# Gathers that add expert rows into the residual, and the norms' two small sums moved from DVE to POOL

## The chip, the cores and the metric

The kernel runs on 1 core of one Trainium2 chip. The metric is the device time of one execution in microseconds; where several executions were timed, it is their median. TensorE (PE) has its own weight loads beside it (PEld). The other engines are VectorE (DVE), ScalarE (ACT), GpSimd (POOL) and SyncE (SP), which here only issues DMAs.

## The reference

Two decoder layers over x, 8 sequences of 256 tokens of 256 numbers, each sublayer followed by a norm. Cut to what matters:

```python
x = _layernorm(x + _L0_attn_ref(x, ...))      # mixing over tokens by a decay matrix
x = _layernorm(x + _L0_xattn_ref(x, ctx_512, ...))   # 16 heads, causal
x = _layernorm(x + _L0_ffn_ref(x, ...))       # 8 experts, top 1, and a shared expert
x = _layernorm(x + _L1_attn_ref(x, ...))      # FFT of the heads, normalized, cumsum, inverse
x = _layernorm(x + _L1_xattn_ref(x, ctx_512, ...))   # 16 heads in a latent space, rope
x = _layernorm(x + _L1_ffn_ref(x, ...))       # ternary weights, gated, rms norm
def _layernorm(x, axis=-1, eps=1e-05):
    m = jnp.mean(x, axis=axis, keepdims=True)
    v = jnp.var(x, axis=axis, keepdims=True)
    return (x - m) / jnp.sqrt(v + eps)
def _L0_ffn_ref(...):
    expert_idx = jnp.argmax(logits, axis=-1)
    for e in range(n_experts):
        out = out + jnp.where(m, h @ down_w[e], 0.0)
    return (out + shared).reshape(S, B, Dm)
```

## The kernel before

A unit is one sequence (256 tokens, two tiles of 128) in one layer. Units 0 to 7 are the first layer, 8 to 15 the second. Five lanes of on-chip buffers hold first-layer units and four lanes hold second-layer units, so that unit u of the second layer uses lane u % 4 and unit 12 takes the buffers of unit 8. Buffers are named after the areas that hold them: "wide" is lanes 0 and 1 of the second layer (and before that the experts' and other weights), "first" is lanes 2 and 3.

Between the layers stand the experts. Each first-layer unit writes its tokens, scaled by the router's score, into the DRAM tensor sent_rows, sorted by expert, and writes its residual plus the shared expert into x_mid (st_mid). When all tokens are sent, 23 tiles of 128 rows are loaded (x_ld), run through the expert of the tile (x_t, x_gu, x_h, x_b, x_dn, x_out) and stored to the DRAM tensor made_rows (x_st). A table of each token's row in made_rows is worked out on DVE (tb_tok).

A second-layer unit then starts. SP loads its rows of x_mid into B.y (ld). POOL issues two indirect DMAs (gt, line 2321), one for each tile of 128 tokens, which gather the tokens' rows of made_rows into B.got. Both wait until all of made_rows and x_mid has landed ("opened"). DVE adds the two (res with n = 0, line 1969) and the norm follows.

A norm (ln, ln_pow, ln_x) is split over three engines. DVE takes the statistics of both tiles (bn_stats, line 1927; bn_aggr, line 1930) into B.mv, whose third column holds eps, then two small reductions give variance + eps (line 1932) and minus the mean (line 1933). POOL raises to the power -0.5 (line 2275) and multiplies (line 2277). ACT applies scale and shift (line 1647). There are 48 norms: two for each first-layer unit (n = 0, 1), four for each of the second layer (n = 0 to 3).

No order is written out by hand. lay_plan describes every part (name, unit, index) with its engine, a length in units of 10 ns, what must come before it, a rank and its PSUM banks. settle(banks, passes, seed) lays all parts out on the engines in simulated time, with a random shake of the ranks by the seed, repeats it for the given number of passes and keeps the layout that ends first. Each engine then runs its parts in that order, and a part waits by semaphores for those before it; an instruction that waits holds up all that stands behind it on its engine. "AIR" is the flight of a DMA. keep_warm puts dummy matmuls (line 1461) into the planned gaps of TensorE of 0.8 us and more, from 9 us on. In the middle of the program the weights of the second layer are prepared: "h" steps fold attention weights (ha is line 1144), "f" steps make the ternary weights (f_sc, f_gt on DVE, f_q on POOL, lines 2332 to 2339).

## Time and profile before

| | us |
|---|---|
| median of 3 runs | 640.63 (639.15 to 644.22) |
| profiled execution | 638.61 |
| its span, first to last instruction | 637.3 |
| mean granted TensorE clock | 0.979 of full speed |

The profile is of one execution. Its span runs from the first to the last instruction; the execution's own time has 1.3 us more around it. Busy time counts an engine's instructions without those that only wait, branch or issue DMAs from SP. TensorE's matmuls overlap, so a duration of one matmul is longer than the step from one to the next. In the tables by stage the busy time of each engine is followed by the number of its instructions; in the order of time a bracket holds the engine's idle time before the instruction and what ended it.

### The profile page before, as it was taken

Reading aid. Unit: us, or ns where it says so; the run is one execution under the profiler, and the core shown is the slowest. Engines: PE = TensorE matmul, PEld = TensorE weight load, DVE = VectorE, ACT = ScalarE, POOL = GpSimd, SP = SyncE. Lnnn points to the kernel's source line nnn. Section 1 sums busy time; section 2 is a strip of 40 time slices with the busy share of each in tenths; the row PEclk is TensorE's granted clock in tenths of the full one; section 3 lists DMA queues with packets and bytes.
Section 4 is the critical chain, followed back from the end, with each engine's and each line's share of the span. In section 5 each row is a group of like instructions: output and inputs, shape, how many; then the busy total and the mean of one; then the engine's idle time right before and its main releaser. Section 6 shows DMA issues by size and latency. Waiting matters only on the chain. (4 is left out here: it accounts for less than half of the span.)

```text
span 637.3 us, 14620 instructions
## 1 busy us (share of the span) xinstructions
PE 574.4 (90%) x5400; PEld 445.5 (70%) x5400; DVE 480.8 (75%) x1286; ACT 386.7 (61%) x826; POOL 374.3 (59%) x468
## 2 busy tenths in 40 slices
PE   5789989988889799876989999999999999999995
PEld 4656767767666465553546888886788768889894
DVE  4673767776688798866779877697988997876656
ACT  3668667667766455541765565665747655655763
POOL 3436445556783267578998654572675634333896
PEclk9999999999899899998989999999999999999999
DMA  9753221102455244426211000001000000000001
GB/s 257 231 147 80 60 84 60 42 19 68 141 145 163 76 124 150 126 92 182 79 38 35 1 2 2 7 29 35 1 9 27 14 21 2 1 2 2 2 1 67
DMA packets 50418, 41.75 MB, mean 66 GB/s; under 512 B 15642, under 2 KB 48924, under 8 KB 50332
## 3 DMA queue, kind: packets, MB, share of 16 engines
q1 hardware_dynamic: 46444, 35.08, 18.6%
q0 software_dynamic: 1536, 4.20, 2.1%
q10 hardware_dynamic: 2368, 1.54, 0.9%
q8 instruction: 44, 0.72, 0.5%
q14 instruction: 26, 0.21, 0.1%
HBM read 31.49 MB, written 10.35 MB: 66 GB/s over the span
## 5 line engine op out<-in xcount | busy, mean ns | idle before, releaser
L1821 DVE TENSOR_TENSOR first<-bank,first 128x512 f16<-128x512 f32 (+3 forms) x141 | 76.1, 556 | 22.5 <-ACT first L1656 5.9
L2297 POOL TENSOR_TENSOR first<-first 128x512 f16<-128x512 f32 x44 | 51.9, 1181 | 42.4 <-ACT first L1708 32.6
L1077 PE MATMUL bank<-c_identity,first 128*128 128x128 f32 (+1 forms) x353 | 58.9, 284 | 9.2 <-DMA first<-in_x 3.1
L1070 PE MATMUL bank<-wide,first 128*128 (+4 forms) x199 | 54.2, 282 | 11.9 <-DVE first L1821 5.1
L1077 PEld LDWEIGHTS bank<-c_identity,first 128*128 128x128 f32 (+1 forms) x353 | 40.3, 141 | 20.3 <-DMA first<-in_x 3.7
L1071 PE MATMUL bank<-wide,first 128*128 (+4 forms) x199 | 53.8, 280 | 0.0
L1072 PE MATMUL bank<-wide,first 128*128 (+4 forms) x199 | 52.9, 279 | 0.0
L2275 POOL TENSOR_TENSOR first<-first,minus_half 128x2 f32<-128x2 f32 x30 | 21.6, 719 | 46.5 <-DVE first L1933 46.5
L1077 PE MATMUL bank<-c_identity,wide 128*128 128x128 f32 (+3 forms) x203 | 34.1, 291 | 9.2 <-DMA c_all_ones<-const_all_ones 7.1
L1821 DVE TENSOR_TENSOR wide<-bank,wide 128x512 f16<-128x512 f32 (+3 forms) x57 | 35.0, 635 | 9.0 <-ACT wide L1687 3.5
L1070 PEld LDWEIGHTS bank<-wide,first 128*128 128x128 f16 (+1 forms) x199 | 19.2, 98 | 24.6 <-issue 16.5
L1647 ACT ACTIVATE wide<-wide 128x256 f32<-128x256 f32 x32 | 17.4, 593 | 31.0 <-POOL wide L2277 30.9
L1077 PEld LDWEIGHTS bank<-c_identity,wide 128*128 128x128 f32 (+3 forms) x203 | 23.9, 146 | 16.2 <-DMA c_all_ones<-const_all_ones 7.1
L1700 ACT ACTIVATE first<-bank 128x512 f16<-128x512 f32 x44 | 26.2, 596 | 11.1 <-PE bank L1328 5.4
L1998 DVE TENSOR_REDUCE first<-bank 128x8 f32<-128x512 f32 x44 | 27.6, 681 | 6.1 <-PE bank L1290 3.7
L2332 POOL TENSOR_TENSOR wide<-wide 128x768 bf16<-128x768 bf16 x8 | 13.1, 1642 | 31.5 <-DVE wide L1919 31.5
L1494 PE MATMUL bank<-first,w_fgu 128*128 128x256 f16 x256 | 29.8, 273 | 0.6 <-DVE first L2219 0.6
L1494 PE MATMUL bank<-wide,w_fgu 128*128 128x256 f16 x256 | 30.1, 273 | 0.0
L2396 POOL TENSOR_TENSOR wide<-wide 128x512 f16<-128x512 f32 x16 | 18.6, 1161 | 19.0 <-ACT wide L1797 19.0
L1708 ACT ACTIVATE first<-bank 128x512 f32<-128x512 f32 x44 | 26.3, 597 | 5.7 <-POOL first L2297 5.5
L2297 POOL TENSOR_TENSOR wide<-wide 128x512 f16<-128x512 f32 x16 | 18.5, 1158 | 17.9 <-ACT wide L1708 15.4
L1070 PE MATMUL bank<-first,wide 128*128 128x256 f16 (+1 forms) x98 | 25.9, 271 | 2.4 <-DVE first L1821 2.4
(471 smaller groups left out, 2106.3 us busy)
## 6 DMA issues: line engine op xcount, KB each, us to landing
first<-sent_rows SPq DMA_DIRECT2D x20, 128.0 KB, 2.0
made_rows<-first SPq DMA_DIRECT2D x20, 128.0 KB, 1.8
wide<-in_L_ffn_gate_w SPq DMA_DIRECT2D x8, 256.0 KB
wide<-in_L_ffn_up_w SPq DMA_DIRECT2D x8, 256.0 KB
wide<-in_L_ffn_down_w SPq DMA_DIRECT2D x8, 256.0 KB
wide<-in_L_xattn_Wq SPq DMA_DIRECT2D x8, 256.0 KB
wide<-in_L_xattn_Wo SPq DMA_DIRECT2D x16, 128.0 KB
wide<-in_L_ffn_w_gate_up SPq DMA_DIRECT2D x8, 256.0 KB
```

The lines of the kernel that those rows point to most:

```text
L1070: mm(o, lhs[0], rhs[0], start=start, stop=False)
L1071: mm(o, lhs[0], rhs[1], start=False, stop=False)
L1072: return mm(o, lhs[1], rhs[0], start=False, stop=stop)
L1077: last = nc.tensor.transpose(view[0:m, c0:c0 + n], src, kc["identity" if dt == F32 else "identity_bf"][0:n, 0:n])
L1494: last = mm(b[:, n * S:(n + 1) * S], k.w_fgu[:, c, at:at + P], B.xT[part][:, c, :], start=(c == 0 and part == 0), stop=(c == C - 1 and par ...
L1700: fn(lane(u).ph[g % 2], scores(u, g)[:, :], ACT.Exp, scale=0.25 if u < NB else 1.0).then_inc(says("ex_h"), 1)
L1708: fn(lane(u).pf, scores(u, g)[:, :], ACT.Exp, scale=0.25 if u < NB else 1.0).then_inc(says("ex_f"), 1)
L1821: return V.tensor_tensor(lo, whole, hi, ALU.subtract)
L1998: V.tensor_reduce(o, b, AX.X, ALU.max).then_inc(says("max_v"), 1)
L2275: pool.step(G.tensor_tensor(B.rstd, B.rstd, k.minus_half, ALU.pow))
L2297: G.tensor_tensor(B.pl[r], B.pf, B.ph[r], ALU.subtract).then_inc(says("ex_l"), 1)
L2396: G.tensor_tensor(lo, B.hf, hi, ALU.subtract).then_inc(says("hf_lo"), 1)
```

## The change

The gathering transfers now add: with compute_op=ALU.add they add the rows of made_rows to what is in B.y. The tile B.got and the addition on DVE (line 1969) go, and the norm waits for the gathers themselves. A gather therefore waits on POOL until its unit's rows of x_mid have landed, and no longer for the addition of the unit that had the lane before. The loads of units 8 and 9 no longer wait for made_rows, but for the experts' last matmuls and for x_mid.

In 44 of the 48 norms DVE stops after bn_aggr; POOL then makes minus the mean (tensor_scalar) and variance + eps (tensor_tensor) ahead of its power. The first norms of units 8 to 11 keep the two reductions on DVE.

The plan's lengths of the norm's parts follow that, and the lengths of f_sc, f_gt, rt_xs, tb_tok and of the gather's flight are changed as well. settle takes 25 passes and seed 157 in place of 37 and 38. Since every engine's order comes out of settle, the order of the whole program is laid out anew.

```diff
@@ -111,6 +111,11 @@
 def was_in(n):
 
     return 3 if n < 3 else 4 if n == 3 else FIRST
+
+
+def sums_on_vector(u, n):
+
+    return NB <= u < NB + LANES and n == 0
 
 
 class Box:
@@ -307,8 +312,8 @@
         p.add(name + "_lo", u, g, lo_on, lo, [(name + "_hi", u, g)], rank)
 
     def norm(u, n, rank, summed="res"):
-        p.add("ln", u, n, "DVE", 130, [(summed, u, n), ("pm_pow", 0, 0)], rank)
-        p.add("ln_pow", u, n, "POOL", 100, [("ln", u, n)], rank)
+        p.add("ln", u, n, "DVE", 130 if sums_on_vector(u, n) else 100, [(summed, u, n), ("pm_pow", 0, 0)], rank)
+        p.add("ln_pow", u, n, "POOL", 100 if sums_on_vector(u, n) else 140, [("ln", u, n)], rank)
         p.add("ln_x", u, n, "ACT", 109, [("ln_pow", u, n)], rank)
 
 
@@ -386,8 +391,8 @@
             p.add("ld_f", 0, i, "SP", 140, freed, rank)
             p.add("in_f", 0, i, "AIR", 350, [("ld_f", 0, i)])
             p.add("f_16", 0, i, "ACT", 82, [("in_f", 0, i)], rank)
-            p.add("f_sc", 0, i, "DVE", 170, [("f_16", 0, i)], rank)
-            p.add("f_gt", 0, i, "DVE", 195, [("f_sc", 0, i)], rank)
+            p.add("f_sc", 0, i, "DVE", 185, [("f_16", 0, i)], rank)
+            p.add("f_gt", 0, i, "DVE", 186, [("f_sc", 0, i)], rank)
             for n2 in range(4):
                 p.add("f_q", 0, 4 * i + n2, "POOL", 164, [("f_q", 0, 4 * i + n2 - 1) if n2 else ("f_gt", 0, i)], rank)
             p.add("fw", 0, i, "PE", 46, [("f_q", 0, 4 * i + 3), ("in_const", 0, 0)], rank, 1, ("fw_c", 0, i))
@@ -444,7 +449,7 @@
         p.add("rt_top", u, 0, "DVE", 20, [("rt", u, 0)], k - 0.5)
         p.add("rt_gate", u, 0, "ACT", 20, [("rt_top", u, 0)], k - 0.5)
         p.add("rt_hot", u, 0, "DVE", 77, [("rt_top", u, 0), old("rk")], k - 0.5)
-        p.add("rt_xs", u, 0, "ACT", 140, [("rt_gate", u, 0)], k - 0.5)
+        p.add("rt_xs", u, 0, "ACT", 114, [("rt_gate", u, 0)], k - 0.5)
         before = [("rk_seen", u - 1, 0)] if u else []
         p.add("rk_seen", u, 0, "DVE", 35, [("rt_hot", u, 0)] + before, k - 0.5)
         p.add("rk", u, 0, "PE", 20, [("rt_hot", u, 0)] + before, k - 0.5, 1, ("rk_slot", u, 0))
@@ -470,7 +475,7 @@
     p.add("tb", 0, 0, "PE", 10, [("rk_seen", NB - 1, 0)], 6, 1, ("tb_cnt", 0, 0))
     p.add("tb_cnt", 0, 0, "DVE", 200, [("tb", 0, 0)] + over, 6)
     p.add("tb_tile", 0, 0, "DVE", 421, [("tb_cnt", 0, 0), ("in_tab", 0, 0)], 6)
-    p.add("tb_tok", 0, 0, "DVE", 498, [("tb_tile", 0, 0)] + [("rk_slot", u, 0) for u in every], 22)
+    p.add("tb_tok", 0, 0, "DVE", 560, [("tb_tile", 0, 0)] + [("rk_slot", u, 0) for u in every], 22)
     for n in range(NT):
         k = 10 + 0.1 * n
         o = n - ELANES if n >= ELANES else None
@@ -499,9 +504,10 @@
             return (name, o, g) if o is not None else None
 
         gate = [("x_in_st", n, 0) for n in range(NT)] + [("in_mid", v, 0) for v in every]
-        p.add("gt", u, 0, "POOL", 200, gate + [("tb_tok", 0, 0), old("res", 0)], k)
-        p.add("in_gt", u, 0, "AIR", 200, [("gt", u, 0)])
-        p.add("ld", u, 0, "SP", 45, gate + [("in_mid", i, 0), old("ln_x", 3)], k)
+        p.add("gt", u, 0, "POOL", 200, gate + [("tb_tok", 0, 0), ("in", u, 0)], k)
+        p.add("in_gt", u, 0, "AIR", 220, [("gt", u, 0)])
+        over = [("x_dn", NT - 1, 0)] + [("in_mid", v, 0) for v in every] if i < 2 else gate
+        p.add("ld", u, 0, "SP", 45, over + [old("ln_x", 3)], k)
         p.add("in", u, 0, "AIR", 250, [("ld", u, 0)])
         p.add("ld_ctx", u, 0, "SP", 90, gate + [old("rope")], k)
         p.add("in_ctx", u, 0, "AIR", 250, [("ld_ctx", u, 0)])
@@ -510,8 +516,7 @@
         p.add("kd_lo", u, 0, "POOL", 43, [("kd_hi", u, 0)], k)
         chain("kt", u, 0, [("rope", u, 0), old("sc", 3)], k, pe=20, hi=29, lo=28)
 
-        p.add("res", u, 0, "DVE", 70, [("in_gt", u, 0), ("in", u, 0)], k)
-        norm(u, 0, k)
+        norm(u, 0, k, "in_gt")
         chain("turn", u, 0, [("ln_x", u, 0)], k)
         for t in range(T):
             p.add("ft", u, t, "PE", 136, [("turn_lo", u, 0), ("pd_lo", 0, 0), ("pd_lo", 0, 1)], k, 1, ("ft_raw", u, t) if t else ("nr", u, 0))
@@ -568,7 +573,7 @@
         p.add("res", u, 3, "DVE", 122, [("rm_pow", u, 0), ("proj", u, 3)], k)
         norm(u, 3, k)
         p.add("st", u, 0, "SP", 45, [("ln_x", u, 3)], k)
-    p.settle(8, 37, 38)
+    p.settle(8, 25, 157)
     p.keep_warm(80, 0.7, 900)
     return p
 
@@ -808,7 +813,7 @@
             return v if dt == F32 else v.bitcast(dt)
 
         tn = "p (t n) -> p t n"
-        B.x, B.y, B.got = (tile([T, D]) for m in range(3))
+        B.x, B.y = (tile([T, D]) for m in range(2))
         B.xT = (tile([C, S], F16), tile([C, S], F16))
         B.ctx, B.kv, B.rot = (tile([DC]) for m in range(3))
         B.kv2 = tile([P])
@@ -988,7 +993,12 @@
                 sp.wait_ge(*done("rt_xs", u - FIRST))
             load(B.x, unit_rows(A["x"], u), dma["x"][u % FIRST])
         else:
-            opened(u)
+            if u < NB + 2:
+                sp.wait_ge(*done("x_dn", NT - 1))
+                for n in range(FIRST):
+                    sp.wait_ge(dma["mid"][n], 16 * turns_of(n))
+            else:
+                opened(u)
             if u >= NB + LANES:
                 sp.wait_ge(*done("ln_x", u - LANES, 3))
             load(B.y, unit_rows(k.x_mid, u - NB), dma["x"][u % LANES])
@@ -1920,7 +1930,10 @@
 
     def ln(u, n):
         B = lane(u)
-        dve.wait_ge(*done("proj" if u < NB and n < 2 else "res", u, n))
+        if u >= NB and n == 0:
+            dve.wait_ge(dma["got"][u % LANES], 32 * visit(u))
+        else:
+            dve.wait_ge(*done("proj" if u < NB and n < 2 else "res", u, n))
         dve.wait_ge(*done("pm_pow", 0))
         y = summed_rows(k, u, n)
         for t in range(T):
@@ -1928,6 +1941,9 @@
         dve.step(last)
         for t in range(T):
             last = V.bn_aggr(B.mv[:, t, 0:2], B.stats[:, t, :])
+        if not sums_on_vector(u, n):
+            last.then_inc(says("ln"), 2)
+            return
         dve.step(last)
         V.tensor_reduce(B.rstd, B.mv[:, :, 1:3], AX.X, ALU.add).then_inc(says("ln"), 1)
         V.tensor_reduce(B.mean, B.mv[:, :, 0:1], AX.X, ALU.add, negate=True).then_inc(says("ln"), 1)
@@ -1963,10 +1979,6 @@
         if u < NB:
             dve.wait_ge(*done("proj", u, n))
             last = V.scalar_tensor_tensor(B.y, bank("proj", u, n)[:, :].rearrange(tn, t=T), 0.5, B.x, ALU.mult, ALU.add)
-        elif n == 0:
-            dve.wait_ge(dma["x"][u % LANES], 16 * (turns_of(u % LANES) + visit(u)))
-            dve.wait_ge(dma["got"][u % LANES], 32 * visit(u))
-            last = V.tensor_tensor(B.y, B.y, B.got, ALU.add)
         elif n < 3:
             dve.wait_ge(*done("proj", u, n))
             last = V.scalar_tensor_tensor(B.y, bank("proj", u, n)[:, :].rearrange(tn, t=T), 1.0, B.x, ALU.mult, ALU.add)
@@ -2272,6 +2284,10 @@
         B = lane(u)
         pool.wait_ge(says("ln"), 2 * k.plan.place[("ln", u, n)] - 1)
         pool.wait_ge(*done("pm_pow", 0))
+        if not sums_on_vector(u, n):
+            pool.wait_ge(says("ln"), 2 * k.plan.place[("ln", u, n)])
+            G.tensor_scalar(B.mean, B.mv[:, :, 0], -1.0, None, ALU.mult)
+            pool.step(G.tensor_tensor(B.rstd, B.mv[:, :, 1], B.mv[:, :, 2], ALU.add))
         pool.step(G.tensor_tensor(B.rstd, B.rstd, k.minus_half, ALU.pow))
         pool.wait_ge(says("ln"), 2 * k.plan.place[("ln", u, n)])
         G.tensor_tensor(B.shift, B.mean, B.rstd, ALU.mult).then_inc(says("ln_pow"), 1)
@@ -2315,11 +2331,10 @@
         B, i = lane(u), u - NB
         opened()
         pool.wait_ge(*done("tb_tok", 0))
-        if u >= NB + LANES:
-            pool.wait_ge(*done("res", u - LANES, 0))
+        pool.wait_ge(dma["x"][u % LANES], 16 * (turns_of(u % LANES) + visit(u)))
         for s in range(T):
-            G.indirect_dma_start(B.got[:, s, :], None, k.made[:, :], bass.IndirectOffsetOnAxis(ap=k.made_at[:, i * T + s:i * T + s + 1], axis=0)
-                                 ).then_inc(dma["got"][u % LANES], 16)
+            G.indirect_dma_start(B.y[:, s, :], None, k.made[:, :], bass.IndirectOffsetOnAxis(ap=k.made_at[:, i * T + s:i * T + s + 1], axis=0),
+                                 compute_op=ALU.add).then_inc(dma["got"][u % LANES], 16)
 
     def f_q(u, n):
         i, step = n // 4, n % 4
```

## Rows read from the trace of the kernel before

**Rows 1.** The page, part 1: busy time, share of the span, instructions.
```profile
PE 574.4 (90%) x5400; PEld 445.5 (70%) x5400; DVE 480.8 (75%) x1286; ACT 386.7 (61%) x826; POOL 374.3 (59%) x468
```

**Rows 2.** Table: stretch, length, busy PE, PEld, DVE, ACT, POOL, clock, DMA, GB/s.
```profile
48.00:208.00 160.00, 142.76 (x1810) 112.64 (x1807) 114.26 (x355) 111.59 (x253) 92.38 (x105) 0.98 0.29 86
208.00:288.00 80.00, 69.33 (x441) 42.27 (x441) 64.31 (x138) 41.84 (x114) 45.40 (x30) 0.98 0.37 111
288.00:304.00 16.00, 10.66 (x44) 5.92 (x44) 10.16 (x27) 3.03 (x8) 14.22 (x14) 0.79 0.62 181
304.00:352.00 48.00, 43.31 (x288) 27.19 (x285) 39.17 (x108) 30.15 (x67) 43.84 (x92) 0.96 0.18 51
352.00:624.00 272.00, 267.28 (x2506) 225.59 (x2505) 214.17 (x555) 169.25 (x321) 153.02 (x176) 1.00 0.03 9
```

**Rows 3.** The same table for line 1461, the dummy matmuls, alone.
```profile
48.00:208.00 160.00, 6.61 (x22) 2.29 (x22) 0.98 0.29 86
...
288.00:304.00 16.00, 4.92 (x23) 2.06 (x21) 0.79 0.62 181
304.00:352.00 48.00, 6.42 (x20) 2.32 (x20) 0.96 0.18 51
```

**Rows 4.** TensorE's waits, 304 to 352 us: total, times, longest.
```profile
PE bank L1476 <- POOL wide L2376: 2.1, 1, 2.1
...
PE bank L1077 <- POOL wide L2385: 0.8, 1, 0.8
```

**Rows 5.** DVE by time: start, duration, instruction, [idle before, until].
```profile
293.31 0.69 DVE L1969 TENSOR_TENSOR wide<-wide 128x512 f32<-128x512 f32 x1 [2.86 <-DMA wide<-made_rows,made_at]
...
294.83 0.25 DVE L1930 BATCH_NORM_AGGREGATE mv<-stats 128x2 f32<-128x6 f32 x2
...
295.19 0.14 DVE L1933 TENSOR_REDUCE wide<-mv 128x2 f32<-128x2 f32 x1
296.02 1.62 DVE L1969 TENSOR_TENSOR wide<-wide 128x512 f32<-128x512 f32 x1 [0.69 <-DMA wide<-made_rows,made_at]
```

**Rows 6.** POOL in order of time, where the second layer begins.
```profile
289.32 1.11 POOL L2321 DMA_INDIRECT wide<-made_rows,made_at  x1 [0.30 <-issue]
...
295.44 1.64 POOL L2332 TENSOR_TENSOR wide<-wide 128x768 bf16<-128x768 bf16 x1
297.04 1.19 POOL L2275 TENSOR_TENSOR wide<-wide,minus_half 128x2 f32<-128x2 f32 x1
...
325.99 1.07 POOL L2321 DMA_INDIRECT wide<-made_rows,made_at  x1 [0.17 <-issue]
...
346.58 0.94 POOL L2321 DMA_INDIRECT first<-made_rows,made_at  x1 [0.30 <-issue]
```

**Rows 7.** TensorE in order of time: the weight fold ahead of unit 8.
```profile
298.26 3.73 PE L1144 MATMUL bank<-wide 128*96 128x256 f32 x8 [5.34 <-DMA wide<-in_L_xattn_W_qr]
```

**Rows 8.** Landing times: gathers (line 2321), loads into lanes 2 and 3.
```profile
DMA to landing us min/median/max: 2.7/3.2/4.5
...
first<-x_mid SPq DMA_DIRECT2D x4, 256.0 KB, 3.7
```

**Rows 9.** Unit 13's load and addition by time; table by stretch.
```profile
434.83 0.36 SPq L897 DMA_DIRECT2D wide<-x_mid  x1
...
438.53 0.68 DVE L1969 TENSOR_TENSOR wide<-wide 128x512 f32<-128x512 f32 x1
...
432.00:464.00 32.00, 29.75 (x251) 22.37 (x250) 26.62 (x73) 22.70 (x47) 17.38 (x21) 1.00 0.06 18
...
507.00:528.00 21.00, 19.68 (x174) 15.10 (x172) 19.02 (x52) 11.81 (x23) 6.96 (x11) 1.00 0.09 26
```

**Rows 10.** The last norm, in order of time.
```profile
632.48 0.25 DVE L1930 BATCH_NORM_AGGREGATE mv<-stats 128x2 f32<-128x6 f32 x2
...
633.00 0.69 POOL L2275 TENSOR_TENSOR first<-first,minus_half 128x2 f32<-128x2 f32 x1 [1.34 <-DVE first L1933]
633.78 0.20 POOL L2277 TENSOR_TENSOR first<-first 128x2 f32<-128x2 f32 x1
```

## The prediction

> **What bounds the kernel now.** I read the engines' busy time first, then a table of busy time by stage, then what ended TensorE's idle time, then the order of time on POOL and DVE where the second layer begins. TensorE is busy for 574.4 of 637.3 us, DVE for 480.8 [rows 1], so whatever is saved must show as TensorE time that is now idle or filled with the dummy matmuls of line 1461. The stages differ widely [rows 2]. From 352 to 624 us TensorE is idle for only 272.0 - 267.28 = 4.7 us: in that stretch less work on DVE or POOL is worth at most that. From 48 to 208 us it is idle for 17.2 us and does 6.6 us of dummies [rows 2, 3]. From 288 to 304 us it is idle for 5.3 us and does 4.9 us of dummies at a granted clock of 0.79, and from 304 to 352 us 4.7 and 6.4 us, while POOL is busy for 43.84 of 48 us [rows 2, 3]. Two of the waits of that last stretch end on POOL, 2.1 and 0.8 us [rows 4]. So the beginning of the second layer is the place where this change can earn something, and POOL is its fullest engine there.
>
> **The change, part by part.** I make the sum against the profiled execution, 638.6 us with a span of 637.3 us; the median of the runs shown is 640.63, 2.0 us more. I carry the difference over to that median.
>
> *The addition in the gather.* Eight DVE additions (line 1969) go. One takes 0.69 us when it runs undisturbed and 1.62 us beside POOL [rows 5]. Eight of them are 5.5 to 13 us of DVE time; off the path they are worth nothing, since TensorE has other work. On the path is the first one: the gathers of unit 8 let it start at 293.31 and its norm starts 0.04 us after it, so the norm may start 0.7 us sooner. There is a second effect. The sums for POOL are ready at 295.33, but POOL took up a ternary-fold step of 1.64 us at 295.44, and the power came at 297.04 and lasted 1.19 us [rows 5, 6]. With the norm 0.7 us sooner the power is ready at 294.6, while POOL is still issuing gathers (until 295.4), and goes before that step if the order says so: 297.04 - 295.44 = 1.6 us. I take 1.6 us in all for the entry. Its bounds: nothing, because TensorE's first matmuls for unit 8 stand behind a weight fold, which waited 5.34 us for a DMA until 298.26; and 5.3 us, that whole wait, if the new order lets the unit's work fill it [rows 7].
>
> The Trainium skill (SBUF — State Buffer, "SBUF: two separate sides") says that a DVE instruction with two SBUF inputs and a POOL instruction that reads SBUF exclude each other for their whole length. The 0.69 against 1.62 us, and the power's 1.19 against 0.69 us, agree with it. By that rule the removed additions also give POOL time back, and the added POOL sums take some from such DVE instructions; neither enters the sum here.
>
> *The gather now waits for its rows' other half, not for an old tile.* Before, the gathers of units 12 to 15 were issued from 325.99 to 347.5 us, in the stretch where POOL is full: 8 issues of about 1.0 us and 0.3 us between the two of a pair, some 9 us [rows 6]. Now each waits for x_mid to land in its lane's tile, which waits for the end of the lane's previous unit (412 us and later). POOL loses 9 of its 43.84 us there. It takes on the sums of the few second norms that fall there, about 1 us. I take the two waits on POOL of rows 4 as what is won, 2.9 us. Bounds: nothing, if what is next is DVE (39.17 of 48 us), and 11.1 us, if all idle and dummy time of this stretch became work [rows 2, 3].
>
> *The price: a lane starts later.* Unit 13's load was issued at 434.83 and its addition began at 438.53, 3.7 us later [rows 9]. Now two gathers follow the load: from the first issue to the landing of the second is 1.3 us to the second issue and 293.31 - 289.32 = 4.0 us from there, 5.3 us; the addition of 0.7 us and its gap go: +4.6 us per lane, plus up to 1.3 us if POOL is busy. It happens at four lanes (units 12 to 15). What covers it is the ready work of the other three lanes. At units 12 and 14 TensorE is full. At units 13 and 15 it is not: it idles 32.0 - 29.75 = 2.25 us from 432 to 464 and 21.0 - 19.68 = 1.3 us from 507 to 528 [rows 9]. If the cover fails, one such start costs 4.6 us. I take a sixth of that at each of the two, 1.5 us together, because even there TensorE waits only in pieces shorter than a restart. Units 10 and 11 load behind the gate as before, and unit 10's gathers come on POOL after four others of some 1.3 us each, longer than the 3.7 us in which its load landed [rows 6, 8]; units 8 and 9 are loaded before the gate. So at the entry the new wait costs nothing. On SP the early loads stand ahead of stores that need a later step of the same tile anyway.
>
> The new wait sits on POOL's queue. Behind it stand the splits, squares and powers of the other three lanes, and TensorE waits for those. The planner gives a load 0.45 + 2.5 us, while the loads of units 10, 11, 14 and 15 took 3.7 us to land [rows 8]: where the order leaves no room, POOL stands still for up to 0.8 us. This is in the 1.5 us, and its failure is part of the third rival.
>
> *What the add itself costs.* No row shows an accumulating transfer. The nearest is the same gather without the add: 2.7 to 4.5 us to landing, 3.2 in the median [rows 8], and about 1 us of POOL per issue. Below: nothing more. Above: the destination is read as well, as long again as a landing, +3.2 us at the entry and at each restart, and POOL's issue doubled. I take nothing more, since a gather of 128 KB is mostly a fixed delay; the upper end goes into the range.
>
> *The small sums.* 44 of 48 norms lose two DVE reductions: from the end of the aggregates to the end of the second reduction, 295.08 to 295.33, 0.25 us of DVE each and 11 us in all [rows 5]. Each gains two POOL instructions of 128x2, like the product at 633.78 (0.20 us), and a wait between, 0.08 us as before that product: 0.35 to 0.48 us, 15 to 21 us in all [rows 10]. On the path of one norm the power began 0.27 us after the aggregates (632.73 to 633.00), now the two instructions and the wait come before it, 0.35 to 0.48 us, and a signal under 0.1 us: about 0.5 us, +0.23 us. In the tail this counts once, and three norms ahead of it on DVE give back 0.17 us or so where they are in series: nothing. In the first layer (13 norms from 48 to 208 us) DVE is busy for 114 and POOL for 92 of 160 us: 3 us less on the fuller, 5 us more on the emptier engine, at most 13 x 0.23 = 3.0 us of latency if no lane covered another. I take nothing; the bounds are -3 and +3 us.
>
> *The order.* The planner gets other durations (also for steps that the code leaves alone: f_sc, f_gt, rt_xs, tb_tok), dependences, seed and passes, so every engine's order is drawn anew. What this does can't be worked out; what it can move can: the 23.9 us idle and dummy from 48 to 208 us and the 10.3 us from 288 to 304 us [rows 2, 3]. I take zero.
>
> Sum: -1.6 - 2.9 + 1.5 = -3.0 us; 638.6 becomes 635.6, and at the level of the median 640.6 - 3.0 = 637.6 us.
>
> **The rivals.**
> *The entry and the new order pay in full.* POOL's freed 9 us and the 5 us of the entry bring 5 and 4 us instead of 2.9 and 1.6, and the order fills a tenth (3 us) of the 34 us above, with 1.5 us of restarts: -10.5 us, 630 us. For it: a fold that waits 5.34 us ahead of ready work is an accident of order. Against it: another accident can take its place.
> *All of it hidden.* TensorE's gaps are refilled by waits on DVE and ACT: 640.6 us. For it: DVE at 39 of 48 us next to POOL.
> *The restarts are exposed (the other side).* At units 13 and 15 the three other lanes run dry and TensorE waits the whole 4.6 us each, 9.2 us, and the two others cost 1 us each: 11.2 - 4.5 = +6.7 us, 647 us. It decides from the point where the three lanes hold less than 4.6 us of ready matmuls at a restart. For it: TensorE waits there already. Against it: from 352 to 624 us all four starts together go with 4.7 us of idle time.
> *The accumulating gather is slow.* The Trainium skill (DMA: Bandwidth & Descriptors, "Rules for kernel authors") says that an accumulating DMA reads its destination and writes it later, so each gather would carry a further trip; no row here can show it. Worked from rows: +3.2 us at the entry and, at two restarts, 3.2 us more each: +9.6 - 3.0 = +6.6 us, again 647 us.
>
> **How the numbers follow.** A measurement of this kernel tells about 1% from no change (6.4 us). Forecast 0.40; paid in full 0.24; all hidden 0.14; restarts exposed or the gather slow 0.22. Faster by over 1% (under 634.2): all but a little of the second case and a part of the forecast's spread, 0.30. Slower (over 647.0): half of the last case and a larger draw of the order, 0.20. Same: 0.50. The range 628 to 648 takes in both neighbours and leaves out an order that moves more than a third of the 34 us. The likeliest case alone spans 634 to 641.
>
> **What would show it.** POOL's busy time from 304 to 352 us falls by some 8 us and its part of TensorE's waits there is gone; no gather stands between unit 11's and 410 us. The first norm of unit 8 starts as its gather lands. Each later lane's first norm starts 8 to 9 us after its load is issued (3.7 before), and TensorE's idle time from there on stays near 5 us; over 10 us there means that the third rival is true. A gather that lands later than 4.5 us after its issue means the fourth. If 48 to 288 us is shorter or longer by more than 3 us, it is the order that has moved the time, and my sum is right or wrong by luck.

## The result and the profile after

The changed kernel is slower. Its time is 1.0095 of the time before (95% interval 1.0073 to 1.0116; medians 648.47 and 642.90 us over 17 runs each). I had forecast 3 us less; it is 6 us more. The profiled execution took 648.99 us, its span is 647.7 us, where the one of before had 637.3.

The page after, part 1, and the stages of the same table as [rows 2] (stretch, length, busy time of PE, PEld, DVE, ACT and POOL with their instructions, granted clock, DMA share, GB/s):

```profile
PE 576.5 (89%) x5398; PEld 445.1 (69%) x5398; DVE 461.7 (71%) x1190; ACT 385.4 (59%) x826; POOL 400.4 (62%) x556
```
```profile
48.00:208.00 160.00, 145.09 (x1785) 112.26 (x1782) 116.00 (x340) 108.77 (x252) 89.54 (x119) 0.99 0.29 86
...
304.00:352.00 48.00, 42.11 (x307) 28.05 (x304) 38.48 (x108) 31.14 (x67) 42.66 (x92) 0.96 0.14 29
352.00:624.00 272.00, 258.03 (x2345) 214.63 (x2344) 196.60 (x483) 158.65 (x304) 157.25 (x212) 0.97 0.06 13
```

DVE has 19 us less work and POOL 26 us more [rows 1]. From 352 to 624 us TensorE is idle for 272.0 - 258.03 = 14.0 us, where it was 4.7 [rows 2], and its mean granted clock there is 0.97, where it was 1.00.

The time was lost late. In POOL's order of time, the first gather of the second layer and the first norm on DVE:

```profile
280.21 1.65 POOL L2336 DMA_INDIRECT wide<-made_rows,made_at  x1 [2.56 <-DMA made_rows<-first]
282.16 1.55 POOL L2336 DMA_INDIRECT wide<-made_rows,made_at  x1 [0.30 <-issue]
...
286.79 0.75 DVE L1940 BATCH_NORM_STATS2 stats<-wide 128x6 f32<-128x256 f32 x2 [1.16 <-DMA wide<-made_rows,made_at]
```

The first gather stands at 280.2 us, where it stood at 288.0:

```profile
288.00 1.02 POOL L2321 DMA_INDIRECT wide<-made_rows,made_at  x1 [1.47 <-DMA made_rows<-first]
```

Until then the changed kernel is 7.8 us ahead in this pair of profiles. From there to the end it takes 647.7 - 280.2 = 367.5 us, before 637.3 - 288.0 = 349.3: 18.2 us more. How far ahead a kernel is at the first gather changes from one execution to the next by some 5 us (the table of places below), so the two numbers are good to about that.

What the gathers' line shows, with the durations of the issue on POOL, and the queue of software-made descriptors on the page (packets, MB, share of 16 engines), first of the kernel after, then of before:

```profile
L2336 POOL DMA_INDIRECT wide<-made_rows,made_at x8: 1537/1600/2130, 280.2 to 456.1; - x8
...
DMA to landing us min/median/max: 3.7/4.0/5.6
```
```profile
q0 software_dynamic: 3072, 4.20, 3.3%
```
```profile
q0 software_dynamic: 1536, 4.20, 2.1%
```

An adding gather keeps POOL for 1.60 us, where a plain one kept it for 1.00, and lands 4.0 us after its issue in the median, where it was 3.2 [rows 8]. The bytes are the same; the packets of that queue have doubled.

### The profile page after: what moved, and what is told of

Its sections match the earlier page's. It is cut to its first block, busy times and chain, and to the rows that moved or that the text cites. A ratio compares the mean times of both kernels' runs of the same rounds, so it can differ in the third digit from the quotient of the medians.

```text
span 647.7 us, 14587 instructions
## 1 busy us (share of the span) xinstructions
PE 576.5 (89%) x5398; PEld 445.1 (69%) x5398; DVE 461.7 (71%) x1190; ACT 385.4 (59%) x826; POOL 400.4 (62%) x556
## 3 DMA queue, kind: packets, MB, share of 16 engines
q1 hardware_dynamic: 46444, 35.08, 18.2%
q0 software_dynamic: 3072, 4.20, 3.3%
q10 hardware_dynamic: 2368, 1.54, 0.9%
## 4 chain that ended last, share of the span: by engine, by line
PE 49%; POOL 14%; DVE 10%; ACT 7%; issue 5%; DMA 4%; SPq 1%; POOLq 0%; DVEq 0%; ACTq 0%
PE bank L1080 8%; PE bank L1082 7%; PE bank L1081 7%; PE bank L1504 6%; PE bank L1087 6%; PE bank L1262 4%; POOL first L2313 2%; POOL first L2336 2%; ACT first L1657 1%; DMA wide<-made_rows,made_at 1%; DVE stats L1940 1%; POOL wide L2336 1%; SPq L902 1%; PE bank L1154 1%; POOL first L2291 1%
## 5 line engine op out<-in xcount | busy, mean ns | idle before, releaser
L1087 PE MATMUL bank<-c_identity,first 128*128 128x128 f32 (+2 forms) x353 | 56.6, 281 | 6.9 <-DVE first L2010 2.3
L1080 PE MATMUL bank<-wide,first 128*128 (+4 forms) x199 | 53.0, 276 | 9.0 <-DVE first L1831 4.2
L1081 PE MATMUL bank<-wide,first 128*128 (+4 forms) x199 | 52.8, 275 | 0.0
L1087 PEld LDWEIGHTS bank<-c_identity,first 128*128 128x128 f32 (+2 forms) x353 | 39.4, 139 | 19.0 <-ACT first L1657 5.9
L1082 PE MATMUL bank<-wide,first 128*128 (+4 forms) x199 | 52.1, 275 | 0.0
L1710 ACT ACTIVATE first<-bank 128x512 f16<-128x512 f32 x44 | 25.9, 594 | 20.5 <-PE bank L1338 11.6
L1504 PE MATMUL bank<-wide,w_fgu 128*128 128x256 f16 x256 | 31.4, 279 | 0.6 <-DVE first L2034 0.6
L1657 ACT ACTIVATE first<-first 128x256 f32<-128x256 f32 x32 | 17.4, 592 | 21.8 <-POOL first L2293 21.8
L2289 POOL TENSOR_SCALAR first<-mv 128x2 f32<-128x2 f32 x28 | 6.9, 248 | 37.9 <-DVE mv L1943 37.8
L2411 POOL TENSOR_TENSOR wide<-wide 128x512 f16<-128x512 f32 x16 | 19.2, 1197 | 17.3 <-ACT wide L1807 17.3
L1504 PEld LDWEIGHTS bank<-wide,w_fgu 128*128 128x128 bf16 x256 | 25.4, 100 | 4.2 <-DVE first L2034 0.9
```

Of the source, the lines that this page charges most:

```text
L1080: mm(o, lhs[0], rhs[0], start=start, stop=False)
L1081: mm(o, lhs[0], rhs[1], start=False, stop=False)
L1082: return mm(o, lhs[1], rhs[0], start=False, stop=stop)
L1087: last = nc.tensor.transpose(view[0:m, c0:c0 + n], src, kc["identity" if dt == F32 else "identity_bf"][0:n, 0:n])
L1504: last = mm(b[:, n * S:(n + 1) * S], k.w_fgu[:, c, at:at + P], B.xT[part][:, c, :], start=(c == 0 and part == 0), stop=(c == C - 1 and par ...
L1657: last = fn(B.x[:, t, :], y[:, t, :], ACT.Identity, bias=B.shift[:, t:t + 1], scale=B.rstd[:, t:t + 1])
```

## The experiments

Each was compared with the kernel before on its own chip, so the ratios are to be compared, not the medians. Names that begin with b_ stand for the kernel before with an edit, those that begin with a_ for the changed kernel with an edit. Every engine keeps the order of that kernel, but for the gathers that b_late, b_add and a_early move on POOL and the addition that b_add takes out of DVE's order. b_seed42, a_told and c_got have orders of their own.

| kernel | ratio to before | 95% interval |
|---|---|---|
| changed | 1.0095 | 1.0073 to 1.0116 |
| b_sums: small sums on POOL | 1.0082 | 1.0051 to 1.0113 |
| b_sums2: the same, second layer only | 1.0023 | 0.9999 to 1.0048 |
| b_late: plain gathers, issued late | 1.0227 | 1.0178 to 1.0277 |
| b_add: adding gathers, issued late | 1.0369 | 1.0315 to 1.0423 |
| b_seed42: another order only | 0.9991 | 0.9955 to 1.0027 |
| a_plain: nothing added | 0.9899 | 0.9864 to 0.9935 |
| a_add8: added for units 8 to 11 only | 0.9952 | 0.9923 to 0.9980 |
| a_got: plain gather to its own tile, DVE adds | 0.9986 | 0.9968 to 1.0004 |
| a_early: the same, gathers early | 0.9983 | 0.9956 to 1.0009 |
| a_vec: changed, sums on DVE | 1.0091 | 1.0063 to 1.0119 |
| a_pad: a_plain with POOL held | 1.0090 | 1.0057 to 1.0124 |
| a_pad_after: the same, behind the pair | 1.0069 | 1.0037 to 1.0100 |
| a_told: the planner knows the gather's lengths | 1.0027 | 1.0007 to 1.0046 |
| c_got: plain gather, sums on POOL, planned anew | 0.9944 | 0.9912 to 0.9975 |

Ratios say what a kernel costs. Where it loses the time is read from places that all the kernels have: the start of the first gather, the start of unit 12's load of x_mid on SP (which waits for the end of unit 8) and the end of the span. One profiled execution of each, in us:

| kernel | first gather | load of unit 12 | end | gather to load | load to end |
|---|---|---|---|---|---|
| before | 288.0 | 412.7 | 637.3 | 124.7 | 224.6 |
| b_late | 292.3 | 413.9 | 659.0 | 121.7 | 245.1 |
| changed | 280.2 | 404.6 | 647.7 | 124.4 | 243.1 |
| a_plain | 283.5 | 402.6 | 633.9 | 119.1 | 231.3 |
| a_add8 | 282.8 | 406.9 | 639.3 | 124.1 | 232.5 |
| a_got | 282.7 | 404.3 | 641.6 | 121.6 | 237.3 |
| a_early | 279.7 | 405.3 | 636.7 | 125.6 | 231.4 |
| a_pad | 283.7 | 409.1 | 646.5 | 125.4 | 237.4 |
| a_pad_after | 285.4 | 410.8 | 645.9 | 125.5 | 235.1 |

b_late runs the same work in the same order as before up to the first gather, and gets there 4.3 us later; the kernels from changed to a_pad_after do the same work up to it, but for a store of a constant, and lie 5.7 us apart. The first column is therefore not to be read as an effect of an edit.

**One part of the change at a time, in the order of before.** b_sums:

```diff
+        if not sums_on_vector(u, n):
+            last.then_inc(says("ln"), 2)
+            return
...
+            G.tensor_scalar(B.mean, B.mv[:, :, 0], -1.0, None, ALU.mult)
+            pool.step(G.tensor_tensor(B.rstd, B.mv[:, :, 1], B.mv[:, :, 2], ALU.add))
```

> The kernel before, in its own order on every engine, with one part of the change: the two small sums of 44 of the 48 norms go from DVE to POOL. Theory 'sums' (they lengthen the norm's path and load POOL): 3 to 6 us slower than before. Theory 'gather' (the adding gather is what costs) and theory 'order' (the new order of all engines is what costs): within 1.5 us of before, with DVE busy about 10 us less and POOL about 20 us more.

It is 0.8% slower, so in this order the theory 'sums' holds. I then left the sums of the first layer on DVE:

```diff
-    return NB <= u < NB + LANES and n == 0
+    return u < NB or (u < NB + LANES and n == 0)
```

> The kernel before in its own order with the small sums on POOL only in the 28 norms of the second layer that the change moves; the 16 norms of the first layer stay on DVE. If each moved norm costs alike: 28 of 44 of the 5.0 us, 3.2 us slower than before. If the cost lies in the first layer, where TensorE waits on short chains (the profile's gate to the second layer came 5.7 us later there): within 1 us of before.

1.0023 is between the two forecasts, 0.5% and nothing. The larger part of the cost seems to come from the 16 norms of the first layer (the intervals of the two kernels, 0.51 to 1.13% and 0.0 to 0.48%, just fail to overlap). The traces can't show where: the first gather moves by 4.3 us without any edit (b_late).

b_add has the other part of the change: adding gathers, waits and loads as in the change, the DVE addition taken out of the order, the gathers of units 12 to 15 moved:

```diff
+        for u in range(NB + LANES, 2 * NB):
+            order = self.order["POOL"]
+            order.remove(("gt", u, 0))
+            landed = self.ends[("in", u, 0)]
+            at = next(n for n, k in enumerate(order) if self.starts[k] >= landed)
+            order.insert(at, ("gt", u, 0))
```

> The kernel before, in its own order, with the other part of the change: the gathers add into B.y, wait for the load of x_mid, and the addition on DVE is gone; the gathers of units 12 to 15 stand on POOL where their load has landed by the plan; the loads of units 8 and 9 wait for the last matmuls of the experts only. Theory 'gather': 5 to 9 us slower than before, with a gather's issue at 1.6 us of POOL and TensorE idle for 10 us or more from 352 to 624 us (before 4.7). Theory 'order': within 2 us of before.

3.7% slower, far more than either theory said. b_late has only the move of the gathers:

> The kernel before, in its own order, but the gathers of units 12 to 15 (still plain, into their own tile, added by DVE) are issued on POOL only where the load of their unit has landed by the plan, instead of at 326 to 347 us. It frees about 9 us of POOL where the second layer begins. If POOL's load there was worth the 2.9 us of the prediction: 2 to 3 us faster than before. If not (the stretch is held by chains that POOL's load doesn't touch): within 1 us. It also holds the late issue alone: slower by 2 us or more would mean that the late gather costs even without the add.

It is itself 2.3% slower. So the late place alone explains most of b_add in an order that was laid out for early gathers. The addition stands in DVE's order where its operands had always been there; now DVE stands still with everything behind it. The line of the addition in b_late:

```profile
its engine sat idle before it (us, times) until:
  DMA first<-made_rows,made_at: 8.3, 3
  DMA wide<-made_rows,made_at: 7.9, 2
```

This is 16.2 us, where the gathers made DVE wait 3.5 us in two waits at the entry before.

Did the relief of POOL that I had counted on come? The busy times of the stretch of [rows 2] in b_late seem to say no:

```profile
304.00:352.00 48.00, 43.46 (x285) 27.19 (x284) 39.15 (x108) 32.03 (x72) 40.07 (x88) 0.97 0.10 29
```

POOL is busy for 3.8 us less than before, TensorE for 0.15 us more. But a busy time holds the dummies too, and does not say how far the kernel has come. The order is the same in both, so the same instruction can be looked up in both. Two of POOL's instructions, one ahead of the gathers' old place and one ahead of unit 12's load, before and then in b_late:

```profile
321.39 0.31 POOL L2347 MEMSET first<- 128x256 bf16 x1
410.58 0.69 POOL L2275 TENSOR_TENSOR wide<-wide,minus_half 128x2 f32<-128x2 f32 x1 [0.43 <-DVE wide L1933]
```
```profile
326.21 0.31 POOL L2365 MEMSET first<- 128x256 bf16 x1
411.80 0.69 POOL L2293 TENSOR_TENSOR wide<-wide,minus_half 128x2 f32<-128x2 f32 x1 [0.43 <-DVE wide L1951]
```

From one to the other it takes 89.19 us before and 85.59 us in b_late: with the gathers gone the stretch is 3.6 us shorter. The relief came, and a little more than the forecast 2.9 us. What b_late loses it loses behind it, 20.5 us from unit 12's load to the end. Looked up in the same way, the loss comes in four steps, one at each restart of a lane: 8.9, 4.0, 4.3 and 3.2 us.

**What the add costs.** a_plain overwrites B.y with the gathered rows; the addition is left out:

```diff
-                                 compute_op=ALU.add).then_inc(dma["got"][u % LANES], 16)
+                                 ).then_inc(dma["got"][u % LANES], 16)
```

> The changed kernel in its order, but the gathers overwrite B.y instead of adding to it, so the expert rows are not added to the residual (that part of the result is left out). All waits and places are those of the changed kernel. It measures what the add itself costs. Theory 'gather, by its price': issue back at 1.0 us of POOL, landing back at about 3.2 us, 3 to 5 us faster than the changed kernel (644 to 645 where the changed one has 648). Theory 'gather, by its place' (the chain load, then gather, is what costs) and theory 'order': within 1.5 us of the changed kernel.

0.9899 against 1.0095: the add in the transfer costs 2.0%, some 12.6 us, more than the theory 'gather, by its price' had said. It is more than the whole loss. a_got does the addition on DVE again; its gathers go to a tile of their own and no longer wait for the load:

```diff
-        pool.wait_ge(dma["x"][u % LANES], 16 * (turns_of(u % LANES) + visit(u)))
+        if u >= NB + LANES:
+            pool.wait_ge(says("ln"), 2 * k.plan.place[("ln", u - LANES, 0)])
...
+            dve.wait_ge(dma["x"][u % LANES], 16 * (turns_of(u % LANES) + visit(u)))
             dve.wait_ge(dma["got"][u % LANES], 32 * visit(u))
+            dve.step(V.tensor_tensor(B.y, B.y, B.got, ALU.add))
```

> The changed kernel in its own order on every engine, but with the addition taken out of the transfer: the gathers stand in the same places of POOL's order, are plain, go to a tile of their own and don't wait for the load; DVE adds the two right ahead of the unit's first norm. Theory 'price of the add' (the issue at 1.6 instead of 1.0 us of POOL and the later landing cost the 13 us that the run without the add regained): 636 to 639 us, of which 1 to 2 us are the eight additions on DVE, so faster than the changed kernel by 1.5 to 2% and faster than before by some 0.6%. Rival 'less work of any kind' (the run without the add was fast because nothing at all was added): 643 us or more.

0.9986: better than the changed kernel by 1.1%, which is less than expected, since the eight additions on DVE, less what the dropped wait may bring, cost 0.9% against a_plain, not 0.2%. With the same order on every engine, the addition is cheaper on DVE than in the transfer. Where the transfer's price arises:

```diff
-                                 compute_op=ALU.add).then_inc(...)
+                                 **({"compute_op": ALU.add} if u < NB + LANES else {})).then_inc(...)
```

> The changed kernel, but only the gathers of units 8 to 11, at the start of the second layer, add; those of units 12 to 15 are plain and their addition is left out. The profiles of the plain and the adding version stand 5 us apart by unit 12's start and 12 us more between there and the end (3.3 of it an earlier gate in one of them). Theory 'it costs at every lane's start': a little over a third of the 2%, 0.996 to 0.999 of the time before. Theory 'it costs at the entry, where POOL is full': 1.004 or more.

0.9952, just below the range of the first theory: of the 2.0% about 0.5% arise at the four starts of the entry and 1.4% at the four restarts. The table of places agrees: from the first gather to unit 12's load the adding gathers take 5.3 us more than plain ones in the changed kernel and 5.0 us in a_add8, and from there to the end 11.8 us, where a_add8, plain again, takes 1.2 us more. It costs at every start, and more at the restarts.

**Issue or landing.** a_pad holds POOL behind each plain gather:

```diff
+            pool.step(G.tensor_tensor(k.pad[1], k.pad[0], k.minus_half, ALU.pow))
```

> The changed kernel with the gathers plain (the addition left out, as in the run that took 0.990 of the time before), and behind each gather's issue a piece of useless POOL work of 0.7 to 0.8 us on tiles of its own. It gives POOL the time of the adding issue (1.6 for 1.0 us), a little more, and the second gather of a pair the same delay, but leaves the transfers plain. Theory 'POOL's time is the price of the add': 1.005 to 1.013 of the time before, nearly all of the 2% between the plain and the adding gather. Theory 'the transfers' own delay is the price' (they land 3.7 us or more after their issue, before 2.7): 0.990 to 0.995.

1.0090 (with the addition left out, as in a_plain and in the next kernel): time on POOL alone brings the whole price back. But the padding delays the second gather too, and in the trace a pair with it takes 1.6 us more of POOL than a plain pair, where the adding pair takes 1.2 us more. So both pieces went behind the second gather:

> As the run with useless POOL work behind each gather's issue (1.009 of the time before), with the same work, but both pieces behind the second gather of a pair, so that the pair is issued and lands as early as the plain one. Theory 'the chain to the landing of the second gather is the price' (0.45 us or more later per pair): back to 0.990 to 0.994. Theory 'POOL's queue is the price' (what stands behind the pair is late by 1.5 us): 1.004 to 1.010.

1.0069: with the pair as early as the plain one, 1.7% are still there. Scaled from 1.6 to 1.2 us a pair, POOL's queue explains about 1.3 of the 2.0%, some 8 us; this is an estimate, and the intervals allow 0.4% either way. The rest is open between the later landing and the width of the intervals.

The restart of unit 14 shows how 0.6 us an issue come out at the end. POOL's order of time in a_plain, then in the changed kernel:

```profile
482.37 1.09 POOL L2336 DMA_INDIRECT first<-made_rows,made_at  x1 [0.17 <-issue]
483.76 0.95 POOL L2336 DMA_INDIRECT first<-made_rows,made_at  x1 [0.30 <-issue]
...
489.54 0.72 POOL L2422 TENSOR_TENSOR first<-first 128x256 f32<-128x256 f32 x1
```
```profile
490.95 1.69 POOL L2336 DMA_INDIRECT first<-made_rows,made_at  x1 [0.18 <-issue]
492.94 1.55 POOL L2336 DMA_INDIRECT first<-made_rows,made_at  x1 [0.30 <-issue]
...
499.31 0.72 POOL L2422 TENSOR_TENSOR first<-first 128x256 f32<-128x256 f32 x1
```

From the first issue to the last sum of another lane's squares: 7.17 us there, 8.36 here, 1.2 us more. Four full-width POOL instructions of other lanes stand between, and none of them makes it up. The third of them, again a_plain first:

```profile
487.08 1.15 POOL L2313 TENSOR_TENSOR wide<-wide 128x512 f16<-128x512 f32 x1
```
```profile
496.26 1.74 POOL L2313 TENSOR_TENSOR wide<-wide 128x512 f16<-128x512 f32 x1
```

TensorE's order of time there, a_plain first as before:

```profile
488.34 0.22 PE L1363 MATMUL bank<-wide 128*128 128x130 f16 x1 [0.47 <-issue]
490.31 0.61 PE L1513 MATMUL bank<-one,first 128*128 128x1 f32 x4 [1.14 <-POOL first L2422]
```
```profile
498.10 0.22 PE L1363 MATMUL bank<-wide 128*128 128x130 f16 x1 [1.65 <-issue]
500.08 1.01 PE L1513 MATMUL bank<-one,first 128*128 128x1 f32 x4 [1.14 <-POOL first L2422]
```

The first of the two gaps has grown by the same 1.2 us. The profile names nothing that ended it, but in both kernels it ends 0.1 us after the POOL instruction above (488.23 and 498.00 us). Then comes a second loss. TensorE's busy time and granted clock in stretches of 4 us, a_plain first:

```profile
487.60:491.60 4.00, 2.39 (x27) 1.00 0.00 0
491.60:495.60 4.00, 3.99 (x43) 1.00 0.00 0
```
```profile
496.00:500.00 4.00, 1.28 (x16) 0.92 0.05 7
500.00:504.00 4.00, 3.92 (x19) 0.50 0.00 0
504.00:508.00 4.00, 4.00 (x33) 0.72 0.00 0
508.00:512.00 4.00, 3.27 (x42) 1.00 0.02 6
```

Behind the longer gaps the granted clock falls to 0.50, the lower level of 1.2 GHz, and is back at 2.4 GHz only after 504 us. By the mean of 0.61 TensorE does 8 x (1 - 0.61) = 3.1 us less in those 8 us. In the changed kernel this happens three times between 416 and 508 us, in a_plain never. Summed over stretches of 4 us from 352 to 624 us, and estimating what the clock takes as each stretch's length times the missing share of the clock, the changed kernel loses 14.0 us to idle time and 6.9 us to the clock, a_plain 9.0 and nothing, a_pad 13.4 and 1.7, a_got 12.1 and 3.4. A fall of the clock is thus not bound to the add: a_pad is as slow as the changed kernel with fewer of them, and a_got has one and is 1.1% faster.

**The chain of load and gather.** a_early is a_got with the plain gathers of units 12 to 15 moved forward on POOL, three pairs to 352 to 359 us and one to 389 us:

```diff
+        for u, ahead in ((12, ("kd_lo", 12, 0)), (13, ("kd_lo", 12, 0)), (14, ("kd_lo", 12, 0)), (15, ("ss", 8, 2))):
+            order.remove(("gt", u, 0))
+            order.insert(order.index(ahead) + 1, ("gt", u, 0))
```

> The kernel with a separate addition on DVE in the order of the changed kernel (it took 0.9986 of the time before), with the gathers of units 12 to 15 issued in POOL's idle time near 355 us instead of behind their loads; they can be, since they go to their own tile. A lane's first norm then waits for the load alone, and no adding transfer is used. Theory 'the chain load, then gather, costs at each restart': 2 to 4 us faster, 0.993 to 0.996 of the time before, and faster than both kernels. Rival 'the order was laid out for the later norm, so an earlier one finds its engines busy': within 1 us, 0.997 to 1.000.

0.9983 beside 0.9986: no gain in sum. But it isn't that nothing happened. The same three instructions of POOL in a_got and then in a_early, one ahead of the gathers' new place, one ahead of unit 12's load, and the last:

```profile
352.38 1.16 POOL L2394 TENSOR_TENSOR first<-first 128x512 f16<-128x512 f32 x1
401.69 0.23 POOL L2291 TENSOR_SCALAR wide<-mv 128x2 f32<-128x2 f32 x1 [2.92 <-DVE mv L1945]
638.12 0.20 POOL L2295 TENSOR_TENSOR first<-first 128x2 f32<-128x2 f32 x1
```
```profile
349.39 1.16 POOL L2407 TENSOR_TENSOR first<-first 128x512 f16<-128x512 f32 x1
402.74 0.23 POOL L2304 TENSOR_SCALAR wide<-mv 128x2 f32<-128x2 f32 x1 [2.90 <-DVE mv L1958]
633.22 0.20 POOL L2308 TENSOR_TENSOR first<-first 128x2 f32<-128x2 f32 x1
```

From the first to the second a_early takes 53.35 us, a_got 49.31: eight gathers on POOL there cost 4.0 us, so its time there was not idle, as I had taken it. From the second to the third it takes 230.48 us, a_got 236.43: the late place had cost 6.0 us. Of these the clock has 1.7 and 3.4 us by the estimate above. So the chain of load and gather does cost at the restarts, 6 us in this order and 20.5 us in one that was laid out for early gathers (b_late), and the early place costs nearly as much on POOL.

**The sums in the changed order.** a_vec takes them back to DVE in all norms:

> The changed kernel in its own order, but all norms' small sums on DVE as before. Theory 'the sums on POOL lengthen each norm' (as in the order of before, where they cost 5 us): 3 to 5 us faster than the changed kernel, 643.5 to 645.5 us. Rival 'this order was laid out for them': within 1.5 us of the changed kernel.

1.0091 beside 1.0095: the rival holds. Here they cost nothing that the intervals show, 0.2 to 0.3% each.

**The order.** b_seed42 changes two numbers:

```diff
-    p.settle(8, 37, 38)
+    p.settle(8, 20, 42)
```

> The kernel before with nothing changed but the seed and the passes of the plan (seed 42, 20 passes): another order of every engine, whose planned end is 645.0 us against 643.6. It measures what a redrawn order alone does. If the plan's end tells the time: 1.002. If an order is worth what I allowed in the prediction (a tenth to a third of the idle time before the second layer): 0.99 to 1.015.

No difference within 0.4%. a_told gives the planner the gather's real lengths:

```diff
-        p.add("gt", u, 0, "POOL", 200, gate + ...)
-        p.add("in_gt", u, 0, "AIR", 220, [("gt", u, 0)])
+        p.add("gt", u, 0, "POOL", 350, gate + ...)
+        p.add("in_gt", u, 0, "AIR", 300, [("gt", u, 0)])
...
-    p.settle(8, 25, 157)
+    p.settle(8, 24, 293)
```

> The changed kernel, with the adding gather's real lengths given to the planner (3.5 us of POOL for the pair and 3.0 us of flight, instead of 2.0 and 2.2) and a seed and passes chosen by the plan's own end. The plan ends at 646.9 us (645.2 by the old lengths, 643.6 for the kernel before). Theory 'the cost is that the order doesn't know the real lengths': 640 to 644 us. Theory 'the cost is in the work and the chain themselves': 646 to 650 us.

1.0027, between the two theories: 0.7% of the time goes when the order knows the lengths, though the plan itself ends 1.7 us later. That it is the lengths and not merely another draw of the order isn't shown; the one draw tried alone (b_seed42) moved nothing. The rest stays in the work.

**A version that beats both.** c_got keeps the sums on POOL, has plain gathers that may be issued early and an addition on DVE as a part of its own, and a plan with measured lengths:

```diff
-        p.add("gt", u, 0, "POOL", 200, gate + [("tb_tok", 0, 0), ("in", u, 0)], k)
-        p.add("in_gt", u, 0, "AIR", 220, [("gt", u, 0)])
+        p.add("gt", u, 0, "POOL", 235, gate + [("tb_tok", 0, 0), old("res", 0)], k)
+        p.add("in_gt", u, 0, "AIR", 200, [("gt", u, 0)])
...
+        p.add("res", u, 0, "DVE", 110, [("in_gt", u, 0), ("in", u, 0)], k)
+        norm(u, 0, k)
...
-    p.settle(8, 25, 157)
+    p.settle(8, 26, 436)
```

> The small sums on POOL as in the change, but the gathers plain, to their own tile and free to be issued early, the addition a part of its own on DVE, and the plan laid out anew with the measured lengths of both (2.35 us of POOL, 2.0 us of flight, 1.1 us of DVE); its planned end is 644.3 us (before 643.6). Theory 'only the adding transfer and lengths that the plan doesn't know cost, the rest is neutral': 0.993 to 1.001 of the time before. Rival 'sums on POOL cost in any order': 1.005 or more.

0.9944: 0.56% faster than before and 1.5% faster than the changed kernel. The rival's 1.005 or more is excluded, so small sums on POOL don't cost in every order. Which of the other parts makes it faster than a_got, the plan's lengths, the early gathers or the draw of the order, isn't separated.

## Why the prediction was wrong, point by point

*The step that failed is "What the add itself costs": I took nothing.* I had both upper ends, +3.2 us of landing and a doubled issue on POOL. Measured, the issue is 1.6 for 1.0 us and the landing 4.0 for 3.2, and together they cost 2.0%, 12.6 us, in the same order (a_plain). Put in for my nothing, they turn the forecast of 3 us less into 9.6 us more; the other terms were off by about 3.5 us in sum the other way. My reason, that such a gather is mostly a fixed delay, looked at the flight only and not at POOL's issue. The fourth rival had the right side and nearly the right size (+6.6 us; +6 measured), but in part by luck: its price for the add was 9.6 us, by landing time at the entry and two restarts, where the add cost 12.6 us, most of it by POOL's queue and at every start.

*The rule of the Trainium skill* on accumulating DMAs (DMA: Bandwidth & Descriptors, "Rules for kernel authors"), that they read their destination and write it later, agrees with the doubled packets and the later landing. That it costs POOL 0.6 us more an issue stands in the run alone.

*The entry, -1.6 us:* wrong. From the second gather's issue to the first norm it takes 286.79 - 282.16 = 4.6 us, before 4.0 to the addition and 4.7 to the norm [rows 5, 6], and the issue ahead of it is 0.6 us longer: from the first issue to the norm 6.6 us, and 6.0 before. The addition's 0.7 us came back as issue and flight. The power of unit 8's first norm, which I had let run ahead of a ternary step, now stands behind unit 9's two gathers:

```profile
290.66 1.33 POOL L2291 TENSOR_TENSOR wide<-wide,minus_half 128x2 f32<-128x2 f32 x1
```

From the first gather to that power it takes 290.66 - 280.21 = 10.5 us, before 297.04 - 288.00 = 9.0 [rows 6]: 1.4 us more, where I had forecast 1.6 us less.

*POOL's relief, -2.9 us:* right in mechanism and size, where it can be isolated: 3.6 us when the gathers leave the stretch in the order of before (b_late), 4.0 us when they come back to it in the changed order (a_early). In the changed kernel itself it can't be told apart. My sign for it failed: POOL's busy time from 304 to 352 us fell from 43.84 to 42.66 us and not by some 8, and TensorE's two waits on POOL there are 2.0 and 0.7 us, as in [rows 4]. With the whole order drawn anew, other work of POOL stands in the gathers' place, so this sign could not decide it.

*The restarts, +1.5 us:* the mechanism was right and the size was not. A norm starts 9.4, 10.5, 12.6 and 9.0 us after its load, where I had said 8 to 9. The late place of the plain gathers costs 6.0 us in the changed order, 3.4 of them by the clock, and in the order of before 20.5 us at all four restarts, not at units 13 and 15 alone. The idle time from 352 to 624 us is 14.0 us, over the 10 us that I had named as the sign of the third rival. That rival is true in part: the chain costs, but with it alone the idle time is 9.0 us (a_plain), and the other 5 us come with the add.

*The sums, 0 us:* within its bounds of 3 us in the changed order (a_vec), beyond them in the order of before (5 us, b_sums). That a norm's latency isn't covered in the first layer was an upper bound (3 us) that I had written down and not taken; that it is the reason is not shown.

*The order, 0 us:* a new seed alone does nothing (b_seed42), yet the first gather stands sooner in all kernels with the changed order (279.7 to 285.4 us) than in those with the order of before (288.0 and 292.3 without an edit ahead of it). Which of the planner's new lengths does that, no run tells. That gain hid a part of the loss behind that point. The prediction had named a shift of over 3 us up to 288 us as the sign that the sum would be right or wrong by luck; it came.

*The granted clock* had no term in the sum. Each gap was counted by its length; three times it brought another 1.7, 1.7 and 3.4 us in the profiled execution.

## What to carry to other kernels

An adding DMA isn't free for the engine that issues it. Price it on the issuer's queue, by what stands behind it there, as well as by its flight: 0.6 us on a busy queue, sixteen times, is 9.6 us of POOL; by the padded kernels some 8 us of it came out at the end, and 12.6 us with the flight. And judge a move inside a fixed order by the time between two instructions that both kernels have, not by the busy time of a fixed stretch: in b_late TensorE's busy time showed 0.15 us and the two instructions 3.6 us. The late place of the same gathers cost 20.5 us in an order laid out for early ones and 6.0 us in one laid out for late ones, so a new place and the order around it have to be judged together.

## What the runs showed of the hardware

An indirect gather of 128 rows of 1 KB with an add takes POOL 1.6 us to issue (1.54 to 2.13), without it 1.0 us (0.95 to 1.11), doubles the packets of its queue (3072 for 1536) and lands at 3.7 to 5.6 us, without it at 2.7 to 4.5 us. Two gaps of 1.65 and 1.14 us within 4 us of TensorE were followed by a granted clock of 0.50 and 0.72 in the next two stretches of 4 us; gaps of 0.47 and 1.14 us at the same place of the program were not.
